# Two query-weight loads ahead of the fifth key-and-value piece in the load order

## The chip, the cores and the metric

The kernel runs on one core of a Trainium2 chip. The metric is the device time of one execution in microseconds (us); three runs of the kernel before gave 2005.05, 2008.74 and 2013.07, so its median is 2008.74.

## The reference, cut to what matters

Two layers of a perceiver-like network: `x` has 256 tokens of width 1024, the context has 4096 tokens. All in float32.

```
x = x + L0_xattn(layernorm(x), ctx)   # 16 query heads of 96, 4 key/value heads; keys from ctx and the latents (4352)
x = x + L0_attn(layernorm(x))         # causal self-attention with rotary embedding
x = x + L0_ffn(layernorm(x))          # top-1 routed low-rank expert
x = x + L1_xattn(layernorm(x), ctx)   # 32 query heads of 32, 8 key/value heads
x = x + L1_attn(layernorm(x))
x = x + L1_ffn(layernorm(x))          # RMS norm, int8-like rounding of activations and weights
```

The change lies at the start of L0_xattn:

```
hidden = concatenate([context, latents], axis=1)      # latents = layernorm(x)
q = (latents @ Wq.T)      # 256 x 1536
k = (hidden @ Wk.T)       # 4352 x 384
v = (hidden @ Wv.T)       # 4352 x 384
```

## The kernel before, in words

Each engine has its own program; the engines meet on semaphores. float32 matrices are split into a high part (ScalarE's cast to fp32r) and a low part (source minus high, on VectorE or GpSimd), and TensorE makes three matmuls for each product: high x high, high x low, low x high.

The stage concerned is `latent_stage` (from line 525), in two phases.

Query phase: 12 rows of queries (`ROWS0`), each 128 rows of the packed query weights against the normed and turned latents. Query panel q (512 KB) is loaded into one of three staging tiles (`queries0`, `queries1`, `between`, in the order i % 3; the trace shows the first two as `queries`). ScalarE casts it (`act_split_query`, L747) into one of three pairs `wq`, once the row three before is made; GpSimd subtracts (L925, raising `wq_split`); TensorE makes 24 matmuls (L649 to L651, raising `q_made`); ScalarE and VectorE take the result out (L771, L774, L778 and L841, raising `q_split`; every third row has one more head, gathered in `fourth`). The trace names the three pairs wq0, wq2, wq1 for rows 0, 1, 2 modulo 3.

Beside two rows of each three (`beside`), ScalarE (L767) and VectorE (L853, raising `w_split`) split one of eight pieces w of the key and value weights (640 KB each), each loaded into one of four staging tiles, i % 4. Beside the last row stand w7 and the two halves c0, c1 of the first context chunk (512 KB each, L723 and L730, raising `c_split`), which use the first two of these four tiles.

Chunk phase: 17 chunks of 256 tokens; TensorE makes their keys and values and the row maxima of the scores (L671 to L703). Before the first, TensorE waits for all rows, all pieces and both halves of the first chunk:

```
pe.wait_ge(*b.q_split.at(ROWS0))
pe.wait_ge(*b.w_split.at(KT))
...
pe.wait_ge(*b.c_split.at(2 * n + 2))
```

SyncE issues the loads one after another in the order of the list `order` (L569 to L572, `load`, L958). Before each it waits until the piece that last used the same staging tile is split: a query load q waits for GpSimd's split of q - 3 (`wq_split`), piece w for VectorE's split of w - 4 (`w_split`), c0 and c1 for w4 and w5, c2 and c3 for c0 and c1. The wait stands at the head of SyncE's program, so everything later in the list waits with it. A piece's tile and its predecessor come from the position among its own kind:

```
z = 4 + i % 3 if what == "q" else i % 4 if what == "w" else i % 2
```

The orders in which ScalarE, VectorE, GpSimd and TensorE take the pieces do not come from `order`; they look up only where a piece has landed (`arrived`). After c3, SyncE sends the low parts of the queries and the turned latents to memory and goes on with the loads of the weight rounding.

Of the kernel before, what the change touches and what calls it, by code (L numbers as in the profile page):

```python
# [74 lines left out]
def flags(kind, names, semaphores):  # L75
    return namedtuple(kind, names)(*[Flag(z) for z in semaphores[:len(names)]])
# [38 lines left out]
def build(nc, a, out):  # L115
# [19 lines left out]
    with ExitStack() as ctx:  # L135
# [3 lines left out]
        def new(stage, names):  # L139
            return [ctx.enter_context(nc.semaphore(f"{stage}_{n}")) for n in names]  # L140
# [4 lines left out]
        c = flags("Cross", CROSS, new("cross", CROSS))  # L145
# [374 lines left out]
        def latent_stage():  # L520
# [44 lines left out]
            for r in range(ROWS0):  # L565
                if r % 3:
                    beside[r].append(("w", r // 3 * 2 + r % 3 - 1))
            beside[ROWS0 - 1] += [("c", 0), ("c", 1)]
            order = [("q", 0), ("q", 1), ("q", 2), ("w", 0), ("w", 1), ("w", 2), ("w", 3), ("q", 3), ("q", 4), ("w", 4),  # L569
                     ("q", 5), ("w", 5), ("q", 6), ("q", 7), ("w", 6), ("q", 8), ("w", 7), ("q", 9), ("q", 10), ("c", 0),  # L570
                     ("q", 11), ("c", 1)]
            order += [("c", half) for half in range(2, 2 * NCH)]  # L572
            place = {piece: n for n, piece in enumerate(order)}

# [479 lines left out]
            return q_low, place_tops, k_sent, v0_sent, v1_sent  # L1054

        q_low, place_tops, *keys_sent = latent_stage()
        panel += [sb(panel_stack, f"panel{i}", [P, KT // 2 * BANK], F32, "right") for i in range(3)]

# [1525 lines left out]
```

## Time and profile before

| | before |
|---|---|
| median of 3 runs | 2008.74 us (2005.05 to 2013.07) |
| profiled execution | 2009.56 us |
| its span, first to last instruction | 2008.2 us |
| mean granted TensorE clock | 0.964 |
| busy in the span: TensorE, VectorE, ScalarE, GpSimd | 93%, 64%, 48%, 26% |

The span is cut into 40 slices of 50.2 us; a digit gives the tenths of a slice that the engine is busy. The changed list governs the first 71 us.

### The profile page before, as it was taken

How to read it: one execution, taken by the hardware profiler on the slowest of the kernel's cores; microseconds unless marked ns; L12 is line 12 of the kernel's file. 1: busy time of each engine (PE TensorE's matmuls, PEld its weight loads, DVE VectorE, ACT ScalarE, POOL GpSimd, SP SyncE). 2: the span in 40 equal slices, each digit the busy share in tenths (PEclk: the TensorE clock that was granted, in tenths of full speed). 3: DMA queues.
4: the chain of work that ended last, by engine and by line, in shares of the span. 5: the costliest groups of instructions: out<-in, count | busy, mean ns of one | idle time of the engine just before them, and what ended most of it. 6: DMA issues, size and time to landing. Idle time of an engine off the chain costs nothing.

```text
span 2008.2 us, 28607 instructions
## 1 busy us (share of the span) xinstructions
PE 1860.0 (93%) x11468; PEld 1349.1 (67%) x11468; DVE 1282.0 (64%) x1504; ACT 959.9 (48%) x1431; POOL 520.6 (26%) x243
## 2 busy tenths in 40 slices
PE   6899999999998999999998987989999999979888
PEld 6899999999997877777787865523333333367543
DVE  4566666665453567887656775757777776156765
ACT  4311133333321777767774351046777667734421
POOL 4100022323200003313100000046777777600000
PEclk9999999999999999999999999979999999988989
DMA  6555688877545568978424526623432321037033
GB/s 239 190 158 169 187 275 230 301 195 247 181 130 145 184 152 225 254 176 212 131 75 146 169 73 153 170 59 83 90 90 67 85 69 33 17 104 276 2 153 124
DMA packets 183939, 302.19 MB, mean 150 GB/s; under 512 B 44077, under 2 KB 117857, under 8 KB 175841
## 3 DMA queue, kind: packets, MB, share of 16 engines
q1 hardware_dynamic: 183809, 300.38, 51.7%
q8 instruction: 91, 1.49, 0.3%
q14 instruction: 39, 0.32, 0.1%
HBM read 232.56 MB, written 64.54 MB: 148 GB/s over the span
## 4 chain that ended last, share of the span: by engine, by line
PE 76%; DVE 14%; ACT 4%; issue 3%; DMA 2%; SPq 1%; POOL 0%; ACTq 0%; DVEq 0%
PE psum L703 11%; PE psum L1915 8%; PE psum L1932 6%; PE psum L684 4%; PE psum L686 4%; PE psum L685 4%; PE psum L671 4%; PE psum L1948 3%; PE psum L302 3%; DVE top L2106 3%; PE psum L304 3%; PE psum L303 3%; PE psum L1896 3%; PE psum L1129 3%; PE psum L1114 2%
## 5 line engine op out<-in xcount | busy, mean ns | idle before, releaser
L2106 DVE TENSOR_REDUCE top<-psum 128x4 f32<-128x2048 f32 (+1 forms) x146 | 294.1, 2026 | 102.4 <-PE psum L1896 102.2
L2031 ACT ACTIVATE probs_f<-psum 128x512 f32<-128x512 f32 x512 | 278.5, 594 | 141.3 <-PE psum L1915 129.1
L2176 POOL TENSOR_TENSOR added<-probs_f 128x1024 f32<-128x1024 f32 x126 | 299.1, 2375 | 171.4 <-ACT probs_f L2031 123.7
L878 DVE TENSOR_REDUCE top<-psum 128x2 f32<-128x512 f32 x272 | 184.8, 690 | 160.3 <-PE psum L671 160.1
L1187 DVE TENSOR_TENSOR probs_low<-probs,probs_high 128x1024 fp32r<-128x1024 f32 x136 | 198.0, 1458 | 127.7 <-ACT probs L1149 127.4
L1915 PE MATMUL psum<-q_rows,k_rows 97*128 97x512 f32 x512 | 197.8, 462 | 2.4 <-DMA q_rows<-t_high 1.7
L1915 PEld LDWEIGHTS psum<-q_rows,k_rows 97*128 97x128 f32 x512 | 80.9, 191 | 173.4 <-ACT probs_f L2031 159.1
L684 PE MATMUL psum<-c_high,w_high 128*128 128x256 f32 (+1 forms) x672 | 190.7, 284 | 2.7 <-DVE c_low L841 2.7
L685 PE MATMUL psum<-c_low,w_high 128*128 128x256 f32 (+1 forms) x672 | 190.4, 283 | 0.0
L686 PE MATMUL psum<-c_high,w_low 128*128 128x256 f32 (+1 forms) x672 | 190.4, 283 | 0.0
L1148 ACT ACTIVATE probs_high<-psum 128x1024 fp32r<-128x1024 f32 x136 | 139.5, 1026 | 84.6 <-PE psum L1116 79.5
L437 POOL TENSOR_TENSOR wf_turned_c<-wf_turned_c,wf_inverse_c 128x1024 f32<-128x1024 f32 (+1 forms) x32 | 74.1, 2318 | 298.2 <-DMA wf_turned_c<-in_ffn_t_dram 298.2
L1932 PE MATMUL psum<-probs_f,v_pair 128*32 128x512 f32 x1024 | 139.9, 619 | 0.2 <-ACT probs_f L2031 0.2
L1149 ACT ACTIVATE probs<-psum 128x1024 f32<-128x1024 f32 x136 | 138.7, 1020 | 0.0
L684 PEld LDWEIGHTS psum<-c_high,w_high 128*128 128x128 f32 (+1 forms) x672 | 128.3, 191 | 2.9 <-DVE c_low L841 2.9
L685 PEld LDWEIGHTS psum<-c_low,w_high 128*128 128x128 f32 (+1 forms) x672 | 128.5, 191 | 0.0
L686 PEld LDWEIGHTS psum<-c_high,w_low 128*128 128x128 f32 (+1 forms) x672 | 128.3, 191 | 0.0
L1129 PE MATMUL psum<-probs_high,value_high 128*128 128x512 f32 x272 | 110.7, 407 | 14.9 <-DVE sums L363 8.8
L703 PE MATMUL psum<-w_high,c_high 128*128 128x384 f32 (+1 forms) x528 | 122.3, 310 | 0.0
L703 PE MATMUL psum<-w_high,c_low 128*128 128x384 f32 (+1 forms) x528 | 122.0, 309 | 0.0
L703 PE MATMUL psum<-w_low,c_high 128*128 128x384 f32 (+1 forms) x528 | 121.9, 309 | 0.0
L1114 PE MATMUL psum<-q_high,key_high 97*128 97x512 f32 x272 | 110.1, 405 | 4.8 <-DMA q_low<-top_low 4.8
(406 smaller groups left out, 3699.9 us busy)
## 6 DMA issues: line engine op xcount, KB each, us to landing
staged<-in_ctxT_dram SPq DMA_DIRECT2D x32, 512.0 KB, 5.5
wf_rows<-in_ffn_w_dram SPq DMA_DIRECT2D x32, 512.0 KB, 6.3
k_four<-k_high SPq DMA_DIRECT2D x128, 128.0 KB, 3.3
wf_rows_c<-in_ffn_w_dram SPq DMA_DIRECT2D x26, 512.0 KB, 4.3
wf_turned_c<-in_ffn_t_dram SPq DMA_DIRECT2D x24, 512.0 KB, 8.1
panel<-in_wo_dram SPq DMA_DIRECT2D x10, 1024.0 KB, 5.9
gate_up<-q_dram SPq DMA_DIRECT2D x10, 1024.0 KB, 7.7
xnT_ab<-in_ffn_t_dram SPq DMA_DIRECT2D x18, 512.0 KB, 6.3
```

The costliest lines, as they stand in the source:

```text
L684: pe.matmul(o, w_high[:, k, col:col + m], high[:, k, :], start=k == 0, stop=False)
L685: pe.matmul(o, w_high[:, k, col:col + m], low[:, k, :], start=False, stop=False)
L686: last = pe.matmul(o, w_low[:, k, col:col + m], high[:, k, :], start=False, stop=k == KT - 1)
L703: last = pe.matmul(o, tokens[:, k, ts], weights[:, k, cols], start=k == 0 and tokens is high and weights is w_high, stop=k == KT - 1 and t ...
L878: dve.tensor_reduce(top0[:, r0:r0 + 2, n], psum[:, bank, :].rearrange("p (i n) -> p i n", i=2), AX_X, ALU.max).then_inc(*b.bank_read.up())
L1129: pe.matmul(o, v_high, p_high, start=sn == 0, stop=False)
L1187: dve.tensor_tensor(probs_low[n % 3][:], probs[n % 2][:], probs_high[n % 3][:].bitcast(F32), ALU.subtract).then_inc(*c.low_set.up())
L1915: pe.matmul(psum[:, half, :], k_rows[kv % 2][:, sn * P:(sn + 1) * P], q_rows[kv % 2][:, half * BANK:(half + 1) * BANK], start=True, stop=T ...
L1932: done = pe.matmul(psum[row:row + HD1, PRODUCTS, :], value, probs[:, (2 * pair + e) % 6, half * BANK:(half + 1) * BANK], start=p == 0, sto ...
L2031: act.activation(probs[:, n % 6, half * BANK:(half + 1) * BANK], psum[:, half, :], ACT.Exp, scale=scale).then_inc(*f.exped.up())
L2106: dve.tensor_reduce(top1[:, first:end, t, chunk], psum[:, MAXIMA + first:MAXIMA + end, :], AX_X, ALU.max).then_inc(*f.max_read.up())
L2176: pool.tensor_tensor(added[pair % 4][:], probs[:, n % 6, :], probs[:, (n + 1) % 6, :], ALU.add).then_inc(*f.added.up())
```

## The change

The list `order` is written anew. The first nine and the last entries keep their places; q5 and q6 come before w4, q7 before w5, q8 and q9 before w6, q10 before w7, q11 before c0.

```diff
-            order = [("q", 0), ("q", 1), ("q", 2), ("w", 0), ("w", 1), ("w", 2), ("w", 3), ("q", 3), ("q", 4), ("w", 4),
-                     ("q", 5), ("w", 5), ("q", 6), ("q", 7), ("w", 6), ("q", 8), ("w", 7), ("q", 9), ("q", 10), ("c", 0),
-                     ("q", 11), ("c", 1)]
+            order = [("q", 0), ("q", 1), ("q", 2), ("w", 0), ("w", 1), ("w", 2), ("w", 3), ("q", 3), ("q", 4), ("q", 5),
+                     ("q", 6), ("w", 4), ("q", 7), ("w", 5), ("q", 8), ("q", 9), ("w", 6), ("q", 10), ("w", 7),
+                     ("q", 11), ("c", 0), ("c", 1)]
             order += [("c", half) for half in range(2, 2 * NCH)]
```

## Rows read from the trace of the kernel before

**Rows 1.** The page: busy tenths in 40 slices.

```profile
PE   6899999999998999999998987989999999979888
```

**Rows 2.** Stretches (us): busy time and instructions by engine, granted clock, DMA share, GB/s.

```profile
core 0: us, PE busy (x) PEld busy (x) DVE busy (x) ACT busy (x) POOL busy (x), PEclk, DMA share, GB/s
...
36.40:49.60 13.20, 10.22 (x72) 10.02 (x72) 6.87 (x7) 7.87 (x12) 7.85 (x4) 0.88 0.55 194
...
100.00:200.00 100.00, 97.46 (x739) 96.16 (x737) 61.18 (x89) 13.37 (x21) 0.00 (x0) 1.00 0.60 165
```

**Rows 3.** Waits from 14 to 71 us: total, times, longest.

```profile
ACT wq1h L747 <- DMA between<-in_wq_dram: 12.3, 3, 4.5
...
PE psum L649 <- POOL wq1l L925: 8.7, 3, 3.1
```

**Rows 4.** Waits of SyncE's queue from 14 to 71 us.

```profile
SPq L958 <- DVE w_low L853: 34.0, 6, 9.0
```

**Rows 5.** The chain of waits in order of time: start us, us, what.

```profile
27.18 1.28 ACT w_high L767
28.49 2.28 DVE w_low L853
30.79 0.33 SPq L958
31.16 4.90 DMA queries<-in_wq_dram
```

**Rows 6.** Timeline of TensorE: start us, us, instruction, idle before and its releaser.

```profile
27.92 0.28 PE L649 MATMUL psum<-x_high,wq0h 128*128 128x256 f32 x1
...
30.80 0.28 PE L649 MATMUL psum<-x_high,wq2h 128*128 128x256 f32 x1
...
36.49 0.58 PE L649 MATMUL psum<-x_high,wq1h 128*128 128x256 f32 x1 [2.66 <-POOL wq1l L925]
...
49.65 0.49 PE L649 MATMUL psum<-x_high,wq1h 128*128 128x256 f32 x1 [2.93 <-POOL wq1l L925]
...
63.41 0.58 PE L649 MATMUL psum<-x_high,wq1h 128*128 128x256 f32 x1 [3.13 <-POOL wq1l L925]
...
70.73 0.58 PE L684 MATMUL psum<-c_high,w_high 128*128 128x256 f32 x1 [2.69 <-DVE c_low L841]
```

**Rows 7.** Timeline of SyncE's queue, the load of q5.

```profile
27.54 0.58 SPq L958 DMA_DIRECT2D between<-in_wq_dram  x1
```

**Rows 8.** Timeline of VectorE.

```profile
25.16 1.99 DVE L853 TENSOR_TENSOR w_low<-staged,w_high 128x1280 fp32r<-128x1280 f32 x1 [0.74 <-ACT w_high L767]
...
35.29 1.43 DVE L841 TENSOR_TENSOR c_high<-fourth,q_high 96x256 fp32r<-96x256 f32 x1
...
39.13 1.82 DVE L853 TENSOR_TENSOR w_low<-staged,w_high 128x1280 fp32r<-128x1280 f32 x1 [0.74 <-ACT w_high L767]
...
66.25 1.49 DVE L853 TENSOR_TENSOR w_low<-staged,w_high 128x1280 fp32r<-128x1280 f32 x1 [0.26 <-ACT w_high L767]
```

**Rows 9.** Timeline of GpSimd.

```profile
18.82 2.38 POOL L925 TENSOR_TENSOR wq1l<-between,wq1h 128x1024 fp32r<-128x1024 f32 x1
23.38 2.41 POOL L925 TENSOR_TENSOR wq0l<-queries,wq0h 128x1024 fp32r<-128x1024 f32 x1 [2.18 <-ACT wq0h L747]
...
34.10 2.35 POOL L925 TENSOR_TENSOR wq1l<-between,wq1h 128x1024 fp32r<-128x1024 f32 x1 [4.68 <-ACT wq1h L747]
37.22 2.38 POOL L925 TENSOR_TENSOR wq0l<-queries,wq0h 128x1024 fp32r<-128x1024 f32 x1 [0.78 <-ACT wq0h L747]
40.12 3.09 POOL L925 TENSOR_TENSOR wq2l<-queries,wq2h 128x1024 fp32r<-128x1024 f32 x1 [0.53 <-ACT wq2h L747]
...
61.01 2.35 POOL L925 TENSOR_TENSOR wq1l<-between,wq1h 128x1024 fp32r<-128x1024 f32 x1 [3.92 <-ACT wq1h L747]
```

**Rows 10.** The tile `queries`, 0 to 110 us: its loads' time to landing.

```profile
DMA to landing us min/median/max: 3.4/5.2/6.2
```

**Rows 11.** Timeline of ScalarE, the cast of q5.

```profile
32.96 1.06 ACT L747 ACTIVATE wq1h<-between 128x1024 fp32r<-128x1024 f32 x1 [4.50 <-DMA between<-in_wq_dram]
```

**Rows 12.** The tile `staged`, 0 to 110 us: its loads' time to landing.

```profile
DMA to landing us min/median/max: 3.5/4.1/11.2
```

## The prediction

> **What bounds the kernel now.** I read the slices of the page first [rows 1]: TensorE, the busiest engine, is at 6 tenths in the first slice (50.2 us each) and at 8 or 9 in nearly all others. The first is where the changed order acts: it holds the loads of the query projection, from 14 us until TensorE starts on the first chunk of the context at 70.73 us. From there on TensorE is full: in 100 to 200 us it is busy 97.46 us at clock 1.00 [rows 2], and what it waits for hangs on its own progress. Nothing there is tied to an absolute time, so whatever moves the start at 70.73 moves the end of the program by as much. The question is how early the first chunk can start.
>
> Next the waits of the stage [rows 3]. TensorE waits three times, 8.7 us in all, for GpSimd's low half of a query panel (L925, tile wq1); behind that stands ScalarE, which waits 12.3 us for the landing of `between`. SyncE's queue, at L958, waits 34.0 us for VectorE's `w_low` [rows 4]: the head of the queue is a key-and-value piece. The chain of waits in order of time [rows 5] shows the loop: ScalarE casts piece 1 (27.18), VectorE makes its low half (28.49), only then SyncE issues a piece (30.79) and behind it the query load (31.16), 4.90 us to land, and ScalarE takes it up. The same four steps come back twice, every three query rows. The period of three query rows is read from TensorE's starts after its waits [rows 6]: 36.49, 49.65, 63.41, so 13.2 and 13.8 us for three rows.
>
> **The change part by part.** Nothing is added or removed: the same 12 query, 8 piece and chunk loads are issued, the one shown in 0.58 us of SyncE's time [rows 7]. No wait of a load changes either, since every piece keeps its staging tile and predecessor. Only which wait stands at the head changes.
>
> Step 1. Load q5 stood behind w4, which waits for the low half of w0 (25.16 + 1.99 = 27.15 on VectorE [rows 8]); it went out at 27.54 [rows 7]. Now it stands behind q4 and needs only the end of GpSimd's third split, 18.82 + 2.38 = 21.20 [rows 9]. Alone in the queue it lands 3.4 us later, the least that this tile's landings show [rows 10], at 24.6. ScalarE reaches it after its cast of w1, 27.18 + 1.28 = 28.46 [rows 5], instead of 32.96, and its 4.50 us wait [rows 11] goes.
>
> Step 2. Load q6 needs the fourth split (23.38 + 2.41 = 25.79 [rows 9]) and goes out there instead of at 31.16, landing by 29.2. ScalarE wants it at about 31. From here on each query load goes out as its staging tile is freed by GpSimd.
>
> Step 3, what is late next. Three candidates per three rows. TensorE: from the start of one row to the next, unhindered, 30.80 - 27.92 = 2.88 us [rows 6], 8.64 for three. ScalarE: busy 7.87 us in the period from 36.4 to 49.6 [rows 2]. The third is GpSimd with VectorE. The rows show that they exclude each other where both read two SBUF tensors. GpSimd's split takes 2.35 alone and 3.09 at 40.12, where VectorE is in a `w_low` until 39.13 + 1.82 = 40.95; it ends at 43.21, 2.26 after that. VectorE's `w_low` takes 1.49 alone; the one at 39.13 ends 1.35 after GpSimd's split ended at 37.22 + 2.38 = 39.60. The small subtraction from `fourth` takes 1.43 at 35.29, ending 0.27 after the split of 34.10 [rows 8, 9]. So three rows cost this pair 3 x 2.26 + 2 x 1.35 + 0.28 = 9.8 us, more than TensorE. The pair is the new pace, not TensorE.
>
> Step 4, the sum. From the end of w1's low half (28.49 + 2.28 = 30.77 [rows 5]) to GpSimd's last split there lie seven splits (q5 to q11), four `w_low` (w2 to w5) and two small subtractions: 7 x 2.26 + 4 x 1.35 + 2 x 0.28 = 15.8 + 5.4 + 0.6 = 21.8. The last split ends at 52.5. Before it ended at 61.01 + 2.35 = 63.36 [rows 9]. What follows it to the chunk's first matmul took 70.73 - 63.36 = 7.4 us, and is VectorE's own list (two `w_low`, the two low halves of the first chunk and five small subtractions), the same after the change. So the chunk starts at 59.9, 10.8 us earlier.
>
> By the Trainium skill, page "SBUF — State Buffer", section "Who interferes with whom", the port that VectorE and GpSimd share is an exclusive lock held for the full instruction. That agrees with who blocks whom above, but with whole durations instead of the held parts the sum would be 7 x 2.35 + 4 x 1.49 + 2 x 0.28 = 23.0, the last split would end at 53.8 and the gain would be 9.6 us.
>
> Step 5, the clock. Over the period from 36.4 to 49.6, which begins behind a gap of 2.66, the granted clock is 0.88 [rows 2, 6]: (1 - 0.88) x 13.2 = 1.6 us of TensorE's work lost, or 3.2 us at the lower level, 1.2 GHz. In the query rows that loss is TensorE's slack, since the chain goes over other engines; it goes with the gaps and is not counted a second time. But the last query row will end at 52.5 + 2.9 = 55.4, and TensorE then waits 4.5 us for the chunk rather than the 2.69 of today [rows 6]. Since 2.66 already costs the clock, the longer wait costs between nothing and another 1.6; it is nearer to the first, and I take 0.3.
>
> Step 6, what is moved later (the times at which ScalarE asks are the rows' durations laid end to end in its own order, held back by GpSimd as in step 4). Pieces w4 to w7 go out behind more query loads. w4's wait ends at 27.15 and q6 ahead of it is out at 25.8, so it goes out as before and lands by 31; ScalarE asks for it near 41.6. w6 and w7 go out near 36.9 and 40.5 (when w2's and w3's low halves and the splits of q6 and q7 are done) and are wanted at 49.6 and 52.9. c0 and c1 still wait for the low halves of w4 and w5; c1 is the tightest, out at about 50.2, landed 3.5 to 4.1 later [rows 12], wanted at about 55. All are covered; were c1's cover gone, it would cost its landing's excess of 1 us or so. The query loads themselves have 0 to 1.5 us to spare at ScalarE, and ScalarE's copy a further 1.5 before GpSimd is free.
>
> Sum: 10.8 - 0.3 = 10.5 us. Against the profiled execution (2009.56, of which the span is 2008.2) this is 1999.1; that execution lies 0.8 above the median of 2008.74, so on the median's footing 1998.2. I predict 1998.3.
>
> **The rivals.**
> (a) TensorE is the pace: VectorE's pieces and GpSimd's splits overlap better than the rows show. Then row 5 starts at 30.8 + 2.9 = 33.7, row 11 at 33.7 + 6 x 2.88 = 51.0, and with 70.73 - 63.41 = 7.3 behind it the chunk starts at 58.3: gain 12.4, 1996.3. For it: TensorE's list is the simplest. Against: every overlapped pair of [rows 8, 9] was blocked.
> (b) The landings pace it in part: if most landings cost the median of 5.2 us and not 3.4 [rows 10], the loop of a tile is 5.2 + 1.06 + 3.1 to 3.6 and hand-overs of 0.3, about 9.9, and with VectorE out of step some 11 for three rows. Seven rows then take 2.6 us longer: gain 7.9 and 2000.8. Against: the 5.2 had a piece or a second query load just ahead; these are now spread.
> (c) The order does little: another wait stands at the head of the queue (w5 before q8, w6 before q10), and the loops only trade places. One of three stalls goes, 4.4 us: 2004.3. Against: those pieces' waits end before the queries' behind them.
> (d) Slower: the pieces, not the queries, arrive late. If each of w4 to w7 landed after ScalarE asks, each would cost a landing of 4.9 and 1.6 of low clock, 26 us in all, and the chunk would start at 86: 2024. It decides once a landing takes over 10 us for w4 or 12 for w6; the longest seen is 11.2 [rows 12], so one is conceivable, four are not.
>
> **How the numbers follow.** Forecast 0.60, (a) 0.15, (b) 0.15, (c) 0.07, (d) 0.03. About 0.5%, or 10 us, is what a measurement of this kernel tells from no change; the runs of before lie between 2005.05 and 2013.07, so the median itself moves by 2 or 3 us. The bound is 1998.7, right at my forecast: half of the forecast's chance, nearly all of (a) and a little of the others give faster 0.47, slower is (d) and a stray 0.01, the rest, 0.49, is within 0.5%. The range goes from (a) less 2 us of such movement to (c): 1994 to 2004.5.
>
> **What would show it.** Steps 1 and 2: query loads issued near 21.2 and 25.8, ScalarE's wait for `between` gone. Step 3: no gap over 1 us on TensorE between 22 and 50, GpSimd's splits mostly at 3.0 or above, VectorE's `w_low` at 1.8 or above. Step 4: last split ends at 52.5, first chunk matmul at 59.9. Step 5: a wait near 4.5 before it. I am wrong if splits stay at 2.4 and TensorE never waits (a), if ScalarE still waits for landings (b), or if the time behind the start does not move along.

## The result and the profile after

Six runs of the changed kernel gave a median of 1992.27 us (1988.89 to 1998.37). Six of the kernel before, the three shown ahead and three beside the change, gave 2006.89 (2003.58 to 2013.07). The ratio is 0.9931 with a 95% interval of 0.9908 to 0.9954, which excludes no change; by the bound of 0.5% that the prediction set this is faster, by one of 2% it would be the same. The forecast was 1998.3 in a range of 1994 to 2004.5, so the time lies 1.7 us below the range.

| | before | after |
|---|---|---|
| profiled execution | 2009.56 us | 1992.85 us |
| its span | 2008.2 us | 1991.2 us |
| mean granted clock | 0.964 | 0.973 |
| row 1 of the queries begins | 21.94 | 22.04 |
| row 11 begins | 63.41 | 53.20 |
| first matmul of the first chunk | 70.73 | 59.88 |
| from there to the end of the span | 1937.5 | 1931.3 |

The timeline of SyncE's queue in the changed kernel, the row that answers to [rows 7] first (start us, us, issue):

```profile
21.33 0.33 SPq L958 DMA_DIRECT2D between<-in_wq_dram  x1
25.92 0.33 SPq L958 DMA_DIRECT2D queries<-in_wq_dram  x1
27.27 0.33 SPq L958 DMA_DIRECT2D staged<-in_wkv_dram  x1
29.55 0.33 SPq L958 DMA_DIRECT2D queries<-in_wq_dram  x1
```

q5 goes out at 21.33 rather than 27.54, q6 at 25.92 rather than 31.16, and w4 between them and q7 at 27.27, when w0's low half is done. On ScalarE, the cast of q5 that waited 4.50 us [rows 11] follows its predecessor at once. What is left of its waits for query landings are four of 0.22 to 1.12 us, two of them shown:

```profile
28.49 1.04 ACT L747 ACTIVATE wq1h<-between 128x1024 fp32r<-128x1024 f32 x1
...
31.37 1.06 ACT L747 ACTIVATE wq0h<-queries 128x1024 fp32r<-128x1024 f32 x1 [0.60 <-DMA queries<-in_wq_dram]
...
44.09 1.06 ACT L747 ACTIVATE wq2h<-queries 128x1024 fp32r<-128x1024 f32 x1 [1.12 <-DMA queries<-in_wq_dram]
```

The waits of SyncE's queue in the same stretch (total, times, longest) show the same thing against the 34.0 us of [rows 4]. Most of what it now waits for is GpSimd's split, the wait that belongs to the query loads themselves:

```profile
SPq L958 <- POOL wq0l L925: 15.2, 3, 8.8
SPq L958 <- DVE w_low L853: 11.3, 6, 5.6
SPq L958 <- POOL wq2l L925: 8.4, 3, 4.5
```

TensorE's timeline answers to [rows 6]. The three gaps of 2.66, 2.93 and 3.13 us are now two of 0.37 and 1.12; the one ahead of the chunk has grown to 3.54:

```profile
42.97 0.38 PE L649 MATMUL psum<-x_high,wq1h 128*128 128x256 f32 x1 [0.37 <-POOL wq1l L925]
...
47.22 0.39 PE L649 MATMUL psum<-x_high,wq0h 128*128 128x256 f32 x1 [1.12 <-POOL wq0l L925]
...
59.88 0.39 PE L684 MATMUL psum<-c_high,w_high 128*128 128x256 f32 x1 [3.54 <-DVE c_low L841]
```

GpSimd and VectorE answer to [rows 8, 9]. The splits from q5 on take 2.60 to 4.29 us, but for the one at 47.13 with 2.40, against 2.35 alone; `w_low` takes up to 3.60:

```profile
29.61 3.53 POOL L925 TENSOR_TENSOR wq1l<-between,wq1h 128x1024 fp32r<-128x1024 f32 x1
33.09 2.60 POOL L925 TENSOR_TENSOR wq0l<-queries,wq0h 128x1024 fp32r<-128x1024 f32 x1
35.66 3.66 POOL L925 TENSOR_TENSOR wq2l<-queries,wq2h 128x1024 fp32r<-128x1024 f32 x1
39.27 3.64 POOL L925 TENSOR_TENSOR wq1l<-between,wq1h 128x1024 fp32r<-128x1024 f32 x1
42.88 4.29 POOL L925 TENSOR_TENSOR wq0l<-queries,wq0h 128x1024 fp32r<-128x1024 f32 x1
47.13 2.40 POOL L925 TENSOR_TENSOR wq2l<-queries,wq2h 128x1024 fp32r<-128x1024 f32 x1
49.48 3.66 POOL L925 TENSOR_TENSOR wq1l<-between,wq1h 128x1024 fp32r<-128x1024 f32 x1
```

```profile
40.92 2.28 DVE L841 TENSOR_TENSOR c_high<-fourth,q_high 96x256 fp32r<-96x256 f32 x1
43.12 0.41 DVE L841 TENSOR_TENSOR c_low<-psum,q_high 96x256 fp32r<-96x256 f32 x1
43.46 1.47 DVE L853 TENSOR_TENSOR w_low<-staged,w_high 128x1280 fp32r<-128x1280 f32 x1
...
47.27 3.60 DVE L853 TENSOR_TENSOR w_low<-staged,w_high 128x1280 fp32r<-128x1280 f32 x1 [0.88 <-ACT w_high L767]
```

So the stage gained 10.85 us, against 10.8 in step 4, while the span fell by 17.0. The other 6.2 us lie behind the start of the chunks. Laying the two executions of TensorE's instructions side by side, the difference stays near 10.7 us to the end of the latent stage (its last TensorE instruction, L712, at 643.0 and 632.3), wanders between 7 and 11 us after it, and jumps by 5 us in one place, where L1915 begins; 1.5 us more come after it. Stretches of that place, first of the kernel before and then of the changed one, aligned at L1915's first matmul (busy time and instructions by engine, granted clock, DMA share, GB/s):

```profile
1313.00:1336.00 23.00, 21.31 (x76) 6.88 (x76) 9.17 (x4) 9.77 (x18) 9.44 (x4) 0.57 0.08 24
```

```profile
1302.50:1325.00 22.50, 20.83 (x109) 7.09 (x109) 11.44 (x6) 12.68 (x24) 11.85 (x5) 0.85 0.08 24
```

TensorE is busy as long in both, but at a granted clock of 0.57 it gets through 76 matmuls, at 0.85 through 109. No load, wait or instruction of the change lies here. Whether the change causes it all the same, or whether it is chance, is what the first experiments ask.

### The profile page after: what moved, and what is told of

It is laid out like the page before. It is cut to its first block, busy times and chain, and to the rows that moved or that the text cites. A ratio compares the mean times of both kernels' runs of the same rounds, so it can differ in the third digit from the quotient of the medians.

```text
span 1991.2 us, 28607 instructions
## 1 busy us (share of the span) xinstructions
PE 1846.3 (93%) x11468; PEld 1339.6 (67%) x11468; DVE 1285.3 (65%) x1504; ACT 959.8 (48%) x1431; POOL 526.0 (26%) x243
## 4 chain that ended last, share of the span: by engine, by line
PE 74%; DVE 16%; ACT 4%; issue 3%; DMA 1%; SPq 1%; POOL 1%; ACTq 0%; DVEq 0%
PE psum L703 11%; PE psum L1915 8%; PE psum L1932 5%; PE psum L686 4%; PE psum L684 4%; PE psum L685 4%; PE psum L671 4%; PE psum L1948 3%; PE psum L302 3%; PE psum L303 3%; PE psum L304 3%; DVE top L2106 3%; DVE probs_low L1187 3%; PE psum L1896 3%; PE psum L1129 2%
## 5 line engine op out<-in xcount | busy, mean ns | idle before, releaser
L1187 DVE TENSOR_TENSOR probs_low<-probs,probs_high 128x1024 fp32r<-128x1024 f32 x136 | 188.1, 1385 | 128.7 <-ACT probs L1149 128.4
L1915 PE MATMUL psum<-q_rows,k_rows 97*128 97x512 f32 x512 | 196.0, 457 | 2.1 <-DMA q_rows<-t_high 1.4
L1915 PEld LDWEIGHTS psum<-q_rows,k_rows 97*128 97x128 f32 x512 | 80.0, 189 | 171.1 <-ACT probs_f L2031 161.4
```

The source lines that it names most:

```text
L1187: dve.tensor_tensor(probs_low[n % 3][:], probs[n % 2][:], probs_high[n % 3][:].bitcast(F32), ALU.subtract).then_inc(*c.low_set.up())
L1915: pe.matmul(psum[:, half, :], k_rows[kv % 2][:, sn * P:(sn + 1) * P], q_rows[kv % 2][:, half * BANK:(half + 1) * BANK], start=True, stop=T ...
```

## The experiments

Theory A: the stage gives 10.8 us or a little more; what is measured beyond it comes from how long the lower clock lasts in later stretches, which differs from execution to execution of one kernel, and the execution and the three runs that the forecast was anchored on were high ones. Theory B: the change itself gives 14 to 17 us. In the stage: the loops through the queue made the stalls, and GpSimd with VectorE is the pace once they are gone; the rivals are the landings and TensorE.

The ratios of before_again, q5_only, after_again and dve_splits_early are taken against 25 runs of the kernel before beside them (median 2004.12), those of after_third and dve_early_again against 23 (median 2005.68). The kernels marked "one run" have a single, profiled execution. "Row 1 to chunk" is from the first matmul of row 1 to the first of the first chunk; "rest" from there to the end of the span.

| kernel | row 1 begins | row 11 begins | chunk begins | row 1 to chunk | rest | ratio to before (95%) |
|---|---|---|---|---|---|---|
| before | 21.94 | 63.41 | 70.73 | 48.8 | 1937.5 | |
| before_again | 19.64 | 63.92 | 71.24 | 51.6 | 1930.9 | 1.0006 (0.9990 to 1.0021) |
| q5_only | 19.73 | 62.06 | 69.38 | 49.7 | 1934.9 | 0.9999 (0.9983 to 1.0014) |
| q5_q6 | 21.04 | 61.27 | 68.59 | 47.6 | 1938.1 | one run |
| dve_splits_old_order | 21.02 | 62.12 | 70.61 | 49.6 | 1935.0 | one run |
| after | 22.04 | 53.20 | 59.88 | 37.8 | 1931.3 | 0.9931 (0.9908 to 0.9954) |
| after_again | 20.94 | 51.61 | 58.30 | 37.4 | 1934.4 | 0.9956 (0.9937 to 0.9974) |
| after_third | 21.06 | 51.71 | 58.40 | 37.3 | 1932.1 | 0.9951 (0.9932 to 0.9971) |
| narrow_low | 22.02 | 52.49 | 59.79 | 37.8 | 1932.3 | one run |
| dve_splits | 21.05 | 49.85 | 56.62 | 35.6 | 1933.5 | one run |
| dve_splits_early | 21.05 | 50.02 | 55.25 | 34.2 | 1938.2 | 0.9920 (0.9899 to 0.9942) |
| dve_early_again | 20.87 | 50.02 | 55.29 | 34.4 | 1935.0 | 0.9930 (0.9907 to 0.9953) |

**before_again**, the kernel before with no edit.

> The kernel before, unchanged, profiled a second time. Theory A (the stage gives 10.8 us, and the rest of the measured difference is the later stretches' granted clock, which varies from execution to execution): the first chunk's matmul starts at 70.7 us again, within 0.2, the last TensorE instruction of the latent stage (L712) near 643.0, but the span can differ from 2008.2 by 3 to 6 us, all of it arising after 643 us in places where the granted clock is at its lower level. Theory B (the change itself gives 14 to 17 us, some of it in later stages): the span comes back within 1 us of 2008.2, and the stretch from 1303 to 1336 us looks as before. Ratio against the kernel before: 1.000 within 0.002 under both.

It ran at the kernel before's own time (1.0006), yet its profiled span is 2002.1, 6.1 us below the first one. The chunk begins at 71.24, within 0.5 us; the rest takes 1930.9 rather than 1937.5. The same stretch, aligned in the same way, has the clock that the changed kernel had:

```profile
1312.20:1335.00 22.80, 21.13 (x109) 7.20 (x109) 11.48 (x6) 12.96 (x24) 11.85 (x5) 0.85 0.09 24
```

That is theory A's: one and the same program gets 0.57 here in one execution and 0.85 in another. L712 came at 644.7, 1.7 us later than in the first, so the latent stage wanders too, by less. I had expected 70.7 within 0.2 and L712 near 643.0. Of the 1.7 us, 1.2 arise behind the chunk's start: in its first 12 us the granted clock is 0.77 with 75 matmuls, where it was 0.88 with 84 in the first execution. The 0.5 before it were not traced back.

**after_again and after_third**, the changed kernel with no edit.

> The changed kernel, unchanged, profiled a second time. Both theories: first chunk's matmul at 59.9, L712 near 632.3. Theory A: over five rounds the ratio comes out at 0.9946 (10.8 us), between 0.9935 and 0.9957, and the span differs from 1991.2 by up to 6 us, from later stretches. Theory B: ratio 0.993 or less (14 us or more), span within 1 us of 1991.2.

> The changed kernel, unchanged, a third time. Theory A (the stage gives 11 to 12 us, the rest of the program takes what its granted clock makes of it): from the first chunk's matmul to the end the span is between 1931 and 1938 us, as in all executions of either order so far; row 1 to the chunk 37.4 to 38; ratio to the kernel before 0.9945, within 0.002. Theory B (the later stages are faster by 3 us or more behind the new order): the rest is 1931 or less and the ratio 0.993 or less.

Ratios 0.9956 and 0.9951, spans 1992.7 and 1990.5, the rest 1934.4 and 1932.1. Both stages took 37.3 to 37.4 us. The chunk began at 58.30 and 58.40 where I expected 59.9; 1.0 to 1.1 us of that is row 1, which began so much earlier than in the first execution. The whole table shows the rest between 1930.9 and 1938.2, and both ends occur behind either order: mean 1935.3 over the five executions with the old order in full or in the main, 1933.8 over the seven with the new. Much of the spread is the place where L1915 begins. after_again shows a third value of the clock there:

```profile
1301.10:1323.60 22.50, 20.74 (x94) 7.11 (x98) 9.42 (x5) 11.94 (x22) 10.68 (x5) 0.73 0.08 23
```

Over all twelve executions, the 22.5 us from L1915's first matmul have one of three clocks, and the time from L1915's first to its last matmul goes with it: 0.58 (75 matmuls) and 440 us in before, dve_splits_old_order, dve_splits_early and dve_early_again, 0.73 (94 to 97) and 437 us in q5_q6 and after_again, 0.84 to 0.85 (109) and 435 us in the other six. Each of the three occurs behind either order. So 4.9 of the 6.2 us are the clock of this one place; the other 1.3 were not traced further.

The gain is in the stage: the chunk starts 10.85 us earlier in the first pair, 12.8 to 12.9 from before_again to after_again and after_third. Over all runs on record, the kernel before has a median of 2004.9 (67 runs, 1996.88 to 2014.29) and the changed one 1994.0 (26 runs, 1988.89 to 2003.24): 10.8 us.

**q5_only**, one part of the change alone.

```diff
-            order = [..., ("w", 3), ("q", 3), ("q", 4), ("w", 4), ("q", 5), ("w", 5), ...
+            order = [..., ("w", 3), ("q", 3), ("q", 4), ("q", 5), ("w", 4), ("w", 5), ...
```

> The old order with q5 alone moved ahead of w4; w5 still stands before q6, w7 before q9, c0 before q11. Theory 1 (the chain of waits runs over w1's low half, the load of w5 and the load of q6 behind it; q5 is not on it): q5 goes out at 21.3, ScalarE's wait for it goes and TensorE's first gap shrinks to under 1 us, but q6 goes out at 31.2 as before, the next gap grows by as much, and the first chunk starts at 70.7, gain 0 within 0.5 us, ratio 1.000. Theory 2 (each query load freed gives its own stall back, as rival (c) counts it): the chunk starts at 66.3, gain 4.4, ratio 0.998.

The ratio is theory 1's: 0.9999, and its interval (0.9983 to 1.0014) just leaves out theory 2's 0.998. The times in the stage are theory 1's only in part: q6 went out at 29.11 and the chunk started at 69.38, where I expected 31.2 and 70.7. Row 1 began 2.2 us earlier than in the first execution, as in before_again; against the two executions of the old order the chunk starts 1.4 and 1.9 us earlier, and row 1 to the chunk lies between theirs. So the gain is at most some 1 to 2 us of the 11. q5 went out at 21.39. TensorE's gap ahead of row 5 is gone and stands ahead of row 6, and ScalarE's longest wait is now for q6. TensorE's and ScalarE's timelines:

```profile
37.61 0.39 PE L649 MATMUL psum<-x_high,wq0h 128*128 128x256 f32 x1 [3.33 <-POOL wq0l L925]
```

```profile
34.07 1.06 ACT L747 ACTIVATE wq0h<-queries 128x1024 fp32r<-128x1024 f32 x1 [5.86 <-DMA queries<-in_wq_dram]
```

The longest stall that one sees (4.50 us for q5) is not the one to remove; [rows 5] already runs through q6.

**q5_q6**, both query loads of the first loop moved ahead of w4.

```diff
-            order = [..., ("q", 4), ("w", 4), ("q", 5), ("w", 5), ("q", 6), ("q", 7), ...
+            order = [..., ("q", 4), ("q", 5), ("q", 6), ("w", 4), ("w", 5), ("q", 7), ...
```

> The old order with q5 and q6 moved ahead of w4; from w5 on as before (w6 before q8, w7 before q9, c0 before q11). Times are taken from the start of row 1 to the first chunk's matmul, since row 0 ends up to 2.3 us earlier or later by the clock granted to it: 48.8 and 51.6 in two executions of the old order, 37.8 and 37.4 of the new. Theory 1 (a stall is a loop of VectorE's low half, a piece's load and the query load behind it, and goes only when the query load at its end no longer stands behind the piece): one of the loops goes, 45 to 47. Theory 2 (only the whole new order helps): 48 or more.

47.6, just above theory 1's range and below theory 2's. It is 1.2 and 4.0 us shorter than the two executions of the old order, whose own difference is 2.8, so one run cannot settle the size; by the chunk's start it is 2.1 and 2.7 us earlier. What stands in the way next is q7, which now goes out behind w4 and w5, at 30.21. ScalarE's timeline:

```profile
37.70 1.06 ACT L747 ACTIVATE wq2h<-queries 128x1024 fp32r<-128x1024 f32 x1 [4.74 <-DMA queries<-in_wq_dram]
```

TensorE's first wait of over 2 us moves to row 7 (2.76 us), and it still waits 3.16 us ahead of row 11. Opening the first loop passes the stall on to the next load behind a piece.

**dve_splits_old_order**, no contention, loads as before. The new part, used by the next kernels as well:

```diff
+                def dve_split_query(r):
+                    w, _ = arrived("q", r)
+                    dve.wait_ge(*b.wq_high_set.at(r + 1))
+                    dve.tensor_tensor(wq[r % 3][1][:], w[:, 0:KT * P], wq[r % 3][0][:].bitcast(F32),
+                                      ALU.subtract).then_inc(*b.wq_split.up())
...
+                    if r + 3 < ROWS0:          # behind w_low, ahead of low_queries
+                        if r == 0:
+                            dve.wait_ge(*b.wq_split.at(3))
+                        dve_split_query(r + 3)
...
-                for r in range(ROWS0):          # GpSimd
+                for r in range(3):
```

> The old order, with the low halves of query panels q3 to q11 made by VectorE in place of GpSimd, so that nothing contends. If the loads' order alone makes the three stalls of before: three waits of TensorE of 2 us or more stay, and row 1 to the chunk takes 43 to 46 us (shorter than 48.8, since the blocked w_low and splits shorten each loop, but far from 37.8). If the contention made them: 38 or less, as in the new order.

49.6 us, as much as the old order takes with the contention. I had expected 43 to 46, thinking that the stretched splits lengthened the loops; one run shows no sign of it, though VectorE also has more to do here, and ScalarE waited 2.42 us for the landing of q6, where it waited 0.82 before. The waits are not quite those expected either: TensorE waits 3.13 and 2.37 us ahead of rows 8 and 11, and 1.35 and 1.58 ahead of rows 5 and 6. With the same edit the new order takes 35.6 (dve_splits, below), so without contention the order of the loads is worth 14.0 us (one run each): it makes the stalls, and the contention is not needed for them.

**narrow_low**, contention halved in the new order.

```diff
+                        cut = slice(0, P if 2 <= k < 6 else 1280)
-                        dve.tensor_tensor(w_low[:, k, :], w[:], w_high[:, k, :].bitcast(F32),
+                        dve.tensor_tensor(w_low[:, k, cut], w[:, cut], w_high[:, k, cut].bitcast(F32),
```

> The new order; VectorE makes the low half of pieces w2 to w5 for 128 of their 1280 columns only (the rest is set to zero by GpSimd before the stage), so this part of the low product is left out. GpSimd keeps all query splits. Four times some 1.2 us of contention go. Pair as pace: GpSimd's splits of q6 to q11 fall from 2.6 to 4.3 us to about 2.5, TensorE's gaps in rows 2 to 11 go, row 1 to row 11 in 28.9 to 29.5 us, chunk 35.5 to 37 after row 1's start. Rivals (a), (b): 31 and 37.5 to 38.

The splits did what was expected of them:

```profile
42.83 2.41 POOL L930 TENSOR_TENSOR wq0l<-queries,wq0h 128x1024 fp32r<-128x1024 f32 x1 [1.56 <-ACT wq0h L747]
45.74 2.41 POOL L930 TENSOR_TENSOR wq2l<-queries,wq2h 128x1024 fp32r<-128x1024 f32 x1 [0.50 <-ACT wq2h L747]
50.06 2.38 POOL L930 TENSOR_TENSOR wq1l<-between,wq1h 128x1024 fp32r<-128x1024 f32 x1 [1.91 <-ACT wq1h L747]
```

but GpSimd now has pauses of 1.56 and 1.91 us, because ScalarE waits for landings:

```profile
41.70 1.06 ACT L747 ACTIVATE wq0h<-queries 128x1024 fp32r<-128x1024 f32 x1 [1.66 <-DMA queries<-in_wq_dram]
48.92 1.06 ACT L747 ACTIVATE wq1h<-between 128x1024 fp32r<-128x1024 f32 x1 [1.17 <-DMA between<-in_wq_dram]
```

Row 11 begins 30.5 us after row 1, against 30.7 to 31.2 in the three executions of the changed kernel and TensorE's 28.8, and the chunk comes no earlier: 37.8. I had expected 28.9 to 29.5 and 35.5 to 37. So the loop split, load, cast stands close behind the pair, and taking away most of the pair's contention alone gives nothing. The landings explain it: the load of q11 goes out at 41.30, 1.6 us before the changed kernel's at 42.94, but ScalarE can take it up only at 48.92, 1.4 us after the changed kernel's 47.51. The median time to landing of the tile `queries` is 4.7 us in the changed kernel and 5.0 here, of `between` 4.5 and 5.8, where I had reckoned with 3.4 for a load on its own. From 38 to 43 us the DMA engines are busy for 0.99 of the time (0.84 in the changed kernel), which would make loads that go out sooner queue for them; no run varies the transfers alone.

**dve_splits**, no contention, shorter splits, new order: the edit of dve_splits_old_order on the changed kernel.

> The new order with VectorE making the low halves of q3 to q11, and w6, w7 where they were (beside rows 10 and 11). If the pair GpSimd and VectorE paces the changed kernel (forecast, step 3): no gap of TensorE above 0.3 us from row 1 to row 11, ten rows of 2.88 us in 28.9 from row 1's start to row 11's, against 31.2 in the changed kernel; chunk 36.0 to 36.5 after row 1's start. If TensorE or the landings already paced it (rivals (a), (b)): 31 and 37.5 to 38 as in the changed kernel.

28.8 us from row 1 to row 11, TensorE without a gap, and 35.6 to the chunk, 0.4 less than the least expected. VectorE's split of 1.22 us takes away the contention and shortens the loading loop as well, by 1.2 us or more a turn. With narrow_low (one run each) this says that pair and loop bound the changed kernel together; TensorE did not, although its rows 2 to 7 follow each other unhindered there (2.88 us each) and are held up from row 8 on.

**dve_splits_early and dve_early_again**, the same with w6 and w7 one row earlier.

```diff
-                    beside[r].append(("w", r // 3 * 2 + r % 3 - 1))
+                    beside[r - (r > 9)].append(("w", r // 3 * 2 + r % 3 - 1))
```

> The changed order, with the low halves of query panels q3 to q11 made by VectorE (1.22 us each for 128 x 1024 by the rows of the chunk's low halves) in place of GpSimd, and w6 and w7 each taken one row earlier (beside rows 9 and 10 in place of 10 and 11). If GpSimd and VectorE excluding each other is the pace of the changed kernel: no w_low above 1.6 us, TensorE without a gap over 0.3 us from row 1 to row 11, row 11 at 51.0 in place of 53.2, and the chunk starts at 56.3 to 57, 3 to 3.5 us before the changed kernel's 59.9: 14 us before the old one, ratio 0.993. If the landings or TensorE set the pace: row 11 at 53 and a chunk start of 59 to 60, ratio 0.9945.

> The new order with VectorE's query splits and w6, w7 one row earlier, a second time: row 1 to the chunk 34.2 us again, 3.5 us less than the changed kernel; the rest 1931 to 1938; ratio to the kernel before 0.9925, within 0.002, and below the changed kernel's in the same call by 0.0015 to 0.002, if the 3.5 us are kept.

Here VectorE makes the splits of the queries (L842) and its `w_low` (L859 in this kernel) is never stretched:

```profile
43.22 1.22 DVE L842 TENSOR_TENSOR wq2l<-queries,wq2h 128x1024 fp32r<-128x1024 f32 x1
44.36 0.41 DVE L847 TENSOR_TENSOR c_low<-psum,q_high 96x256 fp32r<-96x256 f32 x1
44.85 1.49 DVE L859 TENSOR_TENSOR w_low<-staged,w_high 128x1280 fp32r<-128x1280 f32 x1
```

The chunk begins at 55.25 and 55.29, 34.2 and 34.4 us after row 1, 3.0 us or more earlier than in the changed kernel. In the first of the two I had expected row 11 at 51.0 and the chunk at 56.3 to 57; both came about 1 us sooner (50.02, 55.25), as row 1 did. Against dve_splits, 1.2 to 1.4 us of it come from taking w6 and w7 a row earlier, the rest from the splits. The ratios, 0.9920 and 0.9930, lie below those of the changed kernel measured beside them by 0.0036 and 0.0021, with intervals that overlap. Its medians are the lowest of all the kernels, and it leaves nothing of the computation out.

## Why the prediction was right in its steps and wrong in its time

**Steps 1 and 2** were right to 0.13 us: q5 out at 21.33 (21.2), q6 at 25.92 (25.8), ScalarE's casts at 28.49 (28.46) and 31.37 (about 31).

**Step 3** was right about who excludes whom, and only partly about the pace. The pair was stretched as worked out, and GpSimd went from split to split without a pause from 29.61 to 53.14, but the queries' loop through the landings stands level with it (narrow_low, dve_splits). Step 6 gave the loads at ScalarE "0 to 1.5 us to spare"; they overran by 0.60, 0.22, 1.12 and 0.27 us; the median to landing was 4.7 us (`queries`) and 4.5 (`between`) rather than 3.4, and a query load had a piece beside it in most turns. Of the pieces and the halves c0 and c1, none came late: ScalarE waited for none of them.

**Step 4**, the sum: last split's end 53.14 against 52.5, from there to the chunk 6.74 against 7.4, chunk at 59.88 against 59.9. The two small errors cancel, and that the start came out to 0.02 us is luck: the two later executions have it at 58.3 and 58.4. The sum itself held, 22.3 us in the first execution from w1's low half to the last split, and 21.8 in both later ones, where 21.8 was forecast (in these, 0.8 and 0.9 us of it are pauses in which GpSimd waits for ScalarE's casts). The Trainium skill's rule (page "SBUF — State Buffer", section "Who interferes with whom") with whole durations gave 53.8 for the last split, where the two small subtractions were left at their held 0.28 rather than at the 0.41 that one takes alone; with that it gives 54.0. Measured is 53.14, between it and the held parts. Who blocks whom is as the rule says, but for one place (last section).

**Step 5**: the wait before the chunk is 3.54 us rather than 4.5, and the clock cost nothing that can be told: in the chunk's first 12 us the granted clock was 0.86 with 83 matmuls, and 0.88 with 84 in the kernel before. The 0.3 us were not due. Repeats move this more than the change does: 0.77 in before_again, 0.76 and 0.86 in after_again and after_third.

**What failed** is the last step, how the numbers follow. I set the gain of 10.5 us against 2009.56 and 2008.74 and allowed the median of runs 2 to 3 us. That execution had lost some 5 us more than six of the others to the lower clock near 1313 us, and the three runs were high too: over 67 runs the median is 2004.9. From 2004.9 the same sum gives 1994.4, and the changed kernel's median over 26 runs is 1994.0. Of the 6.0 us between the forecast and the result, 3.9 are this start; 1.8 more are the six runs of the result, whose 1992.27 lies below that 1994.0 by chance; the sum's own share is about 0.3. The forecast that the rest of the program moves along rigidly holds as a mean, as far as twelve executions tell (1935.3 and 1933.8), and was wrong for a single one: the rest spreads over 7.3 us. The spread of the three runs (8 us) said as much, and I read it too narrowly; the range should have reached to about 1990. What makes one execution draw 0.57 and another 0.85 at the same place was not tested and stays open; that nothing of the change is needed for it, before_again shows.

Rivals: (a) TensorE as the pace was wrong, 30.7 to 31.2 against 28.8 us for ten rows, although its chunk start of 58.3 was met in the repeats, where row 1 began 1 us earlier; (b) the landings had a share, but no cost in the sum; (c) was wrong for the whole change, and for q5_only even its 4.4 us were too much; (d) did not occur.

## What to carry to other kernels

In a queue of loads in which everything waits behind the first entry, look for the loop in the chain of waits and free every load on it. Freeing the load behind which the longest idle time is seen gave nothing that the runs could tell here, the whole new order 11 us. After that, add up what the engines that block each other have to do between two fixed points; that sum came out within 0.7 us. Before a forecast is set against the time of before, compare the same late stretch in several executions: a single profile and the median of three runs lay 4 to 5 us above the kernel's median, nearly half of the gain.

## What the runs showed of the hardware

- Between GpSimd's and VectorE's instructions that both read two SBUF tensors, the one that has waited longer need not come next. GpSimd's split of q9 was under way from 42.88. The split before it had ended at 42.91 and VectorE's subtraction from `fourth` at 43.20, but the `w_low` that began at 43.46 ran through in 1.47 us, its time alone. GpSimd ended at 47.17, 2.24 us after it. TensorE's gap of 1.12 us follows from this. It is one case: in after_again and after_third the split of q9 was the one that went first.
- The subtraction with one input from PSUM is not held up: 0.41 us at 43.12, beside the split.
- The granted clock of one stretch differs between executions of one program: 0.57 in before and 0.85 in before_again, in some 23 us after L1915 begins (76 and 109 matmuls).
- Row 1 of the queries begins between 19.64 and 22.04 us over all executions. Row 0's matmuls follow each other every 0.21 us in before and every 0.12 in before_again. after_third has both: 12 matmuls in the 2 us from 18 to 20, at a granted clock of 0.50, and 10 in the us from 21 to 22, at 1.00. For before the trace gives a clock of 1.00 with 13 matmuls in the same 2 us, so that its row 0 ran at the lower level is inferred from the spacing and not shown.
